# Index columns of a graph network's gathers and scatters: copied by ScalarE and VectorE instead of GpSimd

## What is computed

```python
edge_index = jnp.stack([src, dst])
h = jnp.maximum(_layernorm(x, axis=-1), 0.0)
x = x + _L0_gnn_ref(h, edge_index, ...)      # attention: softmax over the edges of each dst, tanh
h = jnp.maximum(_layernorm(x, axis=-1), 0.0)
x = x + _L1_gnn_ref(h, edge_index, edge_attr_16, ...)   # second attention, batch norm, gelu
h = jnp.maximum(_layernorm(x, axis=-1), 0.0)
x = x + _L2_gnn_ref(h, edge_index, edge_attr_18, ...)   # attention over the edges of each src
h = jnp.maximum(_layernorm(x, axis=-1), 0.0)
x = x + _L3_gnn_ref(h, edge_weight, ..., src, dst, edge_type_3)   # two rounds of relation sums and a GRU cell
```

```python
e = jax.nn.leaky_relu(a_src[src] + a_dst[dst], NEG_SLOPE)
m = jax.ops.segment_max(e, dst, num_segments=N_NODES)
e = jnp.exp(e - m[dst])
denom = jax.ops.segment_sum(e, dst, num_segments=N_NODES)
alpha = e / (denom[dst] + EPS)
out = jax.ops.segment_sum(alpha[:, None] * h[src], dst, num_segments=N_NODES)
return jnp.tanh(out + bias)
```

## Time and profile before

| | us |
|---|---|
| median of 3 timed runs | 10104.56 |
| lowest and highest | 10097.27, 10124.06 |
| the profiled execution, time | 10032.22 |
| its span in the trace | 10030.5 |

### The profile page before, as it was taken

How to read it: one execution, slowest core, us unless ns; L and a number is a source line. 1 busy time by engine, 2 the same in 40 slices (tenths; PEclk the granted TensorE clock), 3 DMA queues, 4 the chain that set the end, 5 groups by cost and what they waited for, 6 DMA issues and landing times. The chain is left out here.

```text
span 10030.5 us, 76233 instructions
## 1 busy us (share of the span) xinstructions
PE 4389.4 (44%) x11970; PEld 2185.0 (22%) x11970; DVE 5464.7 (54%) x8864; ACT 2292.4 (23%) x4267; POOL 6286.1 (63%) x6569
## 2 busy tenths in 40 slices
PE   0123333334556665000466563333356665776750
PEld 0001111111222222000344341111123332333320
DVE  7766666665666666899111115666633333655554
ACT  0222222222322222333111112222211111222220
POOL 4047777775555555666566666767766666666665
PEclk9999999998555555555555555555566666767765
DMA  5012222222222222333222222222211111111129
GB/s 213 0 48 72 72 72 72 73 73 61 63 63 63 63 63 58 131 140 129 65 66 66 63 66 58 59 59 59 58 48 52 52 52 49 41 41 40 41 73 262
DMA packets 773970, 727.33 MB, mean 73 GB/s; under 512 B 514933, under 2 KB 592334, under 8 KB 769919
## 3 DMA queue, kind: packets, MB, share of 16 engines
q1 hardware_dynamic: 606303, 485.23, 16.4%
q0 software_dynamic: 163104, 216.00, 8.6%
q10 hardware_dynamic: 4512, 25.60, 0.8%
HBM read 433.26 MB, written 309.50 MB: 74 GB/s over the span
## 5 line engine op out<-in xcount | busy, mean ns | idle before, releaser
L706 POOL DMA_INDIRECT l_rows<-in_x,l_num x784 | 831.6, 1061 | 289.9 <-issue 210.4
L706 POOL DMA_INDIRECT l_rows<-xh,l_num x784 | 744.8, 950 | 296.3 <-issue 268.9
L731 POOL DMA_INDIRECT o<-l_out,l_snum x392 | 412.6, 1052 | 537.6 <-DVEq L1184 435.4
L790 PE MATMUL l_p_ea<-all_ident,l_ea 128*32 128x128 f32 x784 | 198.9, 407 | 775.1 <-DMA l_ea<-in_edge_attr 775.1
L731 POOL DMA_INDIRECT g<-l3b_out,l3b_snum x392 | 404.4, 1032 | 206.8 <-issue 187.6
L731 POOL DMA_INDIRECT g<-l3a_out,l3a_snum x392 | 403.4, 1029 | 200.0 <-issue 174.9
L1429 PE MATMUL l_p_qkv<-all_w_qkv,l_hT 128*128 128x128 f32 x784 | 308.9, 498 | 499.8 <-ACT l_hT L1389 335.3
L706 POOL DMA_INDIRECT l2s_rows<-pay,l2s_num x392 | 411.2, 1049 | 184.0 <-issue 105.1
L731 POOL DMA_INDIRECT xh<-l2s_out,l2s_snum x392 | 402.1, 1026 | 187.4 <-issue 123.0
L731 POOL DMA_INDIRECT x<-l_out,l_snum x392 | 393.0, 1003 | 199.0 <-issue 116.0
L706 POOL DMA_INDIRECT l_rows<-x,l_num x392 | 409.7, 1045 | 170.5 <-issue 117.6
(11 more groups left out here) (377 smaller groups left out, 14033.0 us busy)
## 6 DMA issues: line engine op xcount, KB each, us to landing
l_far<-far_d SPq DMA_DIRECT2D x196, 256.0 KB
g<-l_fill SPq DMA_DIRECT2D x194, 256.0 KB
xh<-d_out SPq DMA_DIRECT2D x31, 1600.0 KB, 5.2
pay<-l_out SPq DMA_DIRECT2D x98, 264.0 KB
l2s_far<-far_s SPq DMA_DIRECT2D x98, 256.0 KB
o<-l_fill_o SPq DMA_DIRECT2D x97, 256.0 KB
ts_xin<-in_x SPq DMA_DIRECT2D x31, 800.0 KB, 5.4
x<-ts_row SPq DMA_DIRECT2D x31, 800.0 KB, 4.0
```

What stands on the lines that cost most here:

```text
L706: pool.indirect_dma_start(self.buf[k.u][:, j, at:at + w], None, table, bass.IndirectOffsetOnAxis(ap=self.num[k.u][:, m, j:j + 1], axis=0)) ...
L731: pool.indirect_dma_start(self.table, bass.IndirectOffsetOnAxis(ap=self.num[k.u][:, j:j + 1], axis=0), self.out[k.u][:, j, 0:self.cols], N ...
L790: ins = pe.transpose(self.p[0:32, j * P:(j + 1) * P], self.rows[k.u][:, j, :], c.ident[:])
```

## The change

The index columns are copied by other engines. For the gathers ScalarE does it: first_columns copies those of chunks 0 and 1 at the start of a stage, and next_columns, called in ScalarE's body for chunk n, copies those of chunk n+2 into the tile that chunk n has used. For the scatters VectorE does it, by Scatter.columns, right ahead of the operations that make the result tile. GpSimd keeps its waits (rows_free, num_ready, out_ready) and the transfers; the wait for the old scatter and the semaphore snum_ready go. The diff, cut to one place of each kind:

```diff
@@ class Rows @@
+    def first_columns(self, act):
+
+        for u in range(2):
+            for m, (_, _, _, lst) in enumerate(self.lists):
+                act.activation(self.num[u][:, m, :], lst[:, u * TPC:(u + 1) * TPC], ACT.Copy).then_inc(self.num_ready, 1)
+
+    def next_columns(self, act, c, k):
+
+        if isinstance(k.t, int) and k.t == c.TURNS - 1:
+            return
+        for m, (_, _, _, lst) in enumerate(self.lists):
+            act.activation(self.num[k.u][:, m, :], lst[:, bass.ds((k.i + 2) * TPC, TPC)], ACT.Copy).then_inc(self.num_ready, 1)
+
     def gather(self, pool, k):
         if not k.first:
             hold(pool, self.rows_free, k.n - 2)
-        for m, (_, _, _, lst) in enumerate(self.lists):
-            pool.tensor_copy(self.num[k.u][:, m, :], lst[:, bass.ds(k.i * TPC, TPC)]).then_inc(self.num_ready, 1)
         hold(pool, self.num_ready, k.n * len(self.lists))
@@ class Scatter @@
-        self.snum_ready, self.out_ready = s.sem("snum_ready"), s.sem("out_ready")
+        self.out_ready = s.sem("out_ready")
 
     def scatter(self, pool, k):
-        if not k.first:
-            hold(pool, self.scattered[k.u], 16 * TPC * k.t)
-        pool.tensor_copy(self.num[k.u][:], self.lst[:, bass.ds(k.i * TPC, TPC)]).then_inc(self.snum_ready, 1)
-        hold(pool, self.snum_ready, k.n)
         hold(pool, self.out_ready, k.n)
...
+    def columns(self, dve, step, k):
+
+        step(dve.tensor_copy(self.num[k.u][:], self.lst[:, bass.ds(k.i * TPC, TPC)]))
@@ conv_gat, ScalarE, then VectorE @@
                     if k0:
                         norm.square(act, k0.n)
+                        rows.next_columns(act, c, k0)
...
                         dve.wait_ge(m["tanh_ready"], k2.n)
+                        sct.columns(dve, step, k2)
                         step(dve.scalar_tensor_tensor(sct.out[k2.u][:], r2[:], -2.0, x_one[k2.u][:], ALU.mult, ALU.add))
@@ edge_qkv, ScalarE @@
                     if k:
                         act.wait_ge(m["h_turned"], k.n)
                         act.activation(hT[:], p_hT[:], ACT.Copy).then_inc(m["hT_ready"], 1)
+                        rows.next_columns(act, c, k)
```

More of the change, by code:

```diff
@@ L991, in _ @@
                 load_ln_exp(nc, act)
+                rows.first_columns(act)
                 def body(k0, k1, k2):
```

## The result

The changed kernel is slower: 10198.65 us (median of 4 runs, 10188.01 to 10200.38) against 10106.31 us for the kernel before (4 runs); ratio 1.0087, 95% interval 1.007 to 1.0104. Forecast was 9530. Its profiled execution took 10188.0 us with a span of 10186.3; that of before stood 74 us under its median, so the two profiles differ by 156 us where the medians differ by 92.

What follows compares the result with a forecast made beforehand. GpSimd's transfers and copies were taken to bound four of six stages: -167 - 142 - 137 - 135 + 0 + 0 + 9 = -572 us on 10032, 9460; plus 72 to the median, 9530. Forecast range 9420 to 9620; 9400 to 9780 with (a) and (b).

Steps and rivals of the forecast that it cites:

- I take 0.30: GpSimd-bound stages: without the copies, the gap before a chunk's first gather and first scatter falls from 1.15 to 0.30 us.
- Rival (c): A wait between transfers still costs 0.82 to 0.95 us, so only the copies' time goes: 9945 us; chance 0.12.
- 98 x 1.70 us: First attention stage: two gaps shrink from 1.15 to 0.30 us, chunk from 17.68 to 15.98 us, gaining 167 us.
- an added cost beyond 0.95 is excluded: GpSimd's gap between transfers: at most 0.95 us, since a profiled row already held two waits and a copy's completion.
- With the stops left where they are: Projection stage: rows need 15.4 us, TensorE gets there after 17.6, so ScalarE's later copies stay hidden; gain 0.
- rival (e): Projection stage's stops go if they hang on GpSimd's rhythm; 10.0 us a chunk, 260 us more gain, 9270 us; chance 0.04.
- Rival (d): Projection stage: late index copies make each of 38 stops cost 18 us, not 10; with (c), 10250 us; chance 0.04.
- 0 within 50: Projection stage: GpSimd's 0.85 us saved per chunk set against later index copies; gain 0, bounds 50 us either way.
- 0 within 30: Second attention stage: earlier rows set against VectorE's 0.2 to 0.3 us index copy; change 0, bounds -30 and +30 us.
- (a): Each of 490 new VectorE index copies holds a GpSimd transfer for 0.17 us, 83 us in all: 9610 us; chance 0.05.
- (b): VectorE and TensorE take over in the three late stages at 11.3 us a chunk, halving their gain: 9740 us; chance 0.17.
- Starts (+9): Stage starts: ScalarE's first index copies add 5.6 us in the second attention stage, under 1 us each in five others.

Runs made afterwards that it cites:

- e3: Changed kernel plus GpSimd copying the same columns, at the old places with the old waits, into a buffer nobody reads: 10104.06 us, 1.0002 of the kernel before.
- e5: As e3, but GpSimd waits only for the previous chunk's unused copy, leaving breaks of 0.37 to 0.75 us: 10223.45 us, 1.0122 of the kernel before.
- e7: Who copies chosen by stage; projection stage has ScalarE's columns and a waited unused GpSimd copy before each four gathers: 9900.29 us, 0.9802 of the kernel before.
- e2: Changed kernel with the scatters' index copies and the old-scatter wait back on GpSimd; ScalarE still copies the gathers' columns: 9996.85 us, 0.9884 of the kernel before.
- e4: Kernel before, with ScalarE and VectorE also copying the columns, at the changed kernel's places, into spare buffers nobody reads: 10146.14 us, 1.0044 of the kernel before.
- e1: Changed kernel with the gathers' index copies back on GpSimd; VectorE still copies the scatters' columns: 10166.72 us, 1.0053 of the kernel before.
- e11: Kernel before in every stage but the projection stage, which is that of e7: 9993.85 us, 0.9906 of the kernel before.
- e9: Changed kernel with the first attention stage's scatters on partitions 0 to 63 alone, same number of transfers: 10209.39 us, 1.0135; that stage's stretch 1742 us.
- e6: Changed kernel with SyncE's fills in the first attention stage issued after its loop: stretch 1741 us, 31 stops; whole 10361.97 us, 1.0257.
- e10: Changed kernel with TensorE raising six further semaphore signals a chunk in the first attention stage, three in other softmax stages: 10209.29 us, 1.0135.

## Why the prediction was wrong

**The gap (right).** "I take 0.30" held: 0.31 us before each gather. So did the chunk times built on it in two stages, as far as no stop disturbs them: the lower quartile is 15.6 us where 15.98 was forecast and 10.7 for 10.9 in the softmax. In the recurrent stages it is 11.2, half a microsecond over the 10.6 and 10.8. Rival (c), the gap stays, is out. On the sequencer that runs ahead the rule of the Trainium skill ("Perfetto Trace Analysis", DMA Instruction, SWDGE) and this trace agree.

**The step that failed** is the first sentence of the part on GpSimd's stages, that removed are "the copies and the trip from a copy through a semaphore to the next transfer", counted as dead time, 98 x 1.70 us and so on. I priced what GpSimd does without them and not what the others do: without the breaks TensorE's signals came late (41, 18, 48 and 46 times in the four stages, 0 before). e3 and e5 show it with the columns filled in the new way both times: with the 1.15 us breaks no stops in these stages and 1.0002, with 0.37 to 0.75 us the stops and 1.0122. The bound "an added cost beyond 0.95 is excluded" was right for the gap and was used for the whole edit. The forecast took GpSimd's row of transfers to be limited by GpSimd alone. No run kept a stage under 1.443 us per transfer, by breaks or by stops, and before, these stages stood at 1.474 (17.68 / 12) to 1.583 already. If that least is a limit, which no run shows, the first attention stage had from 17.68 to 1.45 x 12 = 17.4 us a chunk to give, an estimated 27 us and not 167. It isn't the whole account: by it the recurrent stages too would have gained, and they lost 78 and 65 us at 1.60 per transfer. There the late signals, 247 and 229 us in sum, lie in the chain that the prediction itself named (rows, TensorE, ScalarE, TensorE, scan).

**A rival that no run tests.** The record of the semaphores thins out in the same places. Of VectorE's updates in the first attention stage 97% are in the trace of before and 90% in that of e3, but 40% in the changed kernel and 42% in e5. All executions here were recorded, each with its span and granted clock. Whether the recording itself has a part in making signals late, and so in the loss, stays open.

**Stops taken as fixed.** The earlier trace rows held the sign: stops only in the one stage where 8 transfers a chunk had a single break of 1.15 us; its chunks without a stop took 10.9 us, 1.36 per transfer. "With the stops left where they are" and rival (e), "if they hang on GpSimd's rhythm", are the places. (e) had the right link and the wrong direction: the closer rhythm took no stops away (29 to 45 by their count; the late signals stayed about as many, 50 and 48), and the two breaks of e7 made them milder. Rival (d), the slower case, looked for the loss in the projection stage, by ScalarE's late index copies. GpSimd does wait for them (249.7 us, 48 times, all but one in this stage), and the stage still is 8 us shorter, as the forecast's 0 within 50 says.

**Second attention stage (size wrong).** 0 within 30 was forecast, +36 came. e2, with VectorE's copy gone, has 16.41 us a chunk; e3, e4 and e1, with it, 16.76 to 16.80, the changed kernel 16.75. The windows (busy by engine; granted clock, DMA share and GB/s last) of the changed kernel and, below, of e2:

```profile
3000.00:3300.00 300.00, 187.44 (x458) 77.75 (x456) 190.32 (x313) 89.46 (x173) 146.18 (x142) 0.50 0.23 61
```

```profile
3000.00:3300.00 300.00, 179.97 (x469) 76.97 (x467) 191.76 (x306) 91.69 (x179) 154.69 (x162) 0.57 0.24 63
```

The copy takes 0.17 us; the kernels with it have 16.74 to 16.80 us a chunk, those without it 16.35 to 16.41. TensorE's granted clock differs too, 0.50 (the level of 1.2 GHz throughout) against 0.57, but it isn't the cause, as two windows of e4 show:

```profile
2600.00:2800.00 200.00, 110.23 (x308) 48.26 (x306) 127.41 (x214) 58.46 (x117) 112.81 (x118) 0.67 0.23 59
3600.00:3800.00 200.00, 124.70 (x300) 51.66 (x300) 127.82 (x211) 60.91 (x119) 112.29 (x116) 0.50 0.25 63
```

At 0.67 and at 0.50 the chunk takes the same 17.05 us. What was mis-sized is the term of 0.2 to 0.3 us for VectorE's index copy, and the gain of up to 0.3 us a chunk that was set against it didn't come.

**The other rivals.** (a), VectorE's copies hold GpSimd's transfers, didn't come: the first stage's gathers take 956 ns in the median, 975 before. (b), VectorE and TensorE take over, would show in the chunks without a stop. Those of the softmax are at the forecast (10.7 us against 10.9); those of the recurrent stages, at 11.2, are near the 11.3 that (b) named, so it may be a part of it. Its price was added up wrongly: at 11.3 us the three stages gain 103, 69 and 86 us, 258 and not 210.

**Starts (+9).** +26 came, 11 of them ahead of the second attention stage and 10 ahead of the last recurrent one.

**Chances.** 0.94 for faster hung on a sum of four terms with one common assumption; that GpSimd's rate is GpSimd's own was never given a rival on the slower side. The sign that was named, a new idle group ahead of GpSimd's gathers, was one place off: it came ahead of the scatters (227.4 us).

## What to carry to other kernels

Before you take short work off an engine that issues transfers back to back, ask what uses the breaks: look for waits whose releaser has long been done ("remote" here), count the transfers between them, and divide each stage's time by its transfers. If stages with different work stand at about the same time per transfer (1.47 to 1.58 us in five of the six here), suspect a limit that they share: closing the gaps may then only turn them into stops of some 10 us that hit the engines behind. In such a case a break of 1 us placed ahead of every four transfers can be a gain (e7, e11), and which engine fills the index columns is worth deciding by stage.

## What the runs showed of the hardware

- With GpSimd's indirect transfers 0.30 us apart, TensorE's signals come late: after some 30 of them in a row ScalarE started 9.47 us after the start of TensorE's turning in place of 1.15, and the semaphore changed 8.3 us after the turning's end. No signal of VectorE or ScalarE was late so. Rows gathered meanwhile arrive as usual: VectorE's first use of them follows the last gather's start by 2.3 to 3.1 us in each chunk in which it waits for them.
- No stage of these runs fell under 1.443 us per indirect transfer, and leaving out half of the rows in a third of the transfers (e9) didn't lower the first attention stage's 1.485.
- SyncE's requests last 0.70 us in place of 0.33 to 0.38 meanwhile. The Trainium skill ("Perfetto Trace Analysis", DMA Instruction, HWDGE) says that this duration holds the wait for a lock, the making of the descriptors and the push of a semaphore; which of the three grows, the rows don't tell. What GpSimd's transfers, SyncE's requests and TensorE's signals share was not found: half of SyncE's requests in the stage (e6), a sixth of the rows (e9) and more signals from TensorE (e10) made no difference.
- A copy of 4 columns on VectorE took 0.17 us and cost the second attention stage 0.38 us a chunk. A chunk there took 17.05 us at a granted clock of 0.67 and of 0.50 (e4).
